# A mixture-of-experts block on one core: attention without loops, expert outputs scattered by token, late routing on VectorE

## The reference, cut to what matters

```
h = x + attention(rmsnorm(x))            # 16 heads of 8 channels, softmax over 1024 keys
out = h + moe(rmsnorm(h))                # 8 experts, top 2 of 8 logits per token, softmax of the two
moe: for each chosen expert e of a token:
       y = (silu(xf @ w1[e].T) * (xf @ w3[e].T)) @ w2[e].T      # 128 -> 256 -> 128
       out += weight * y
```

## Time and profile before

| what | value |
|---|---|
| three runs | 1239.31, 1238.51, 1228.23 us (median 1238.51) |
| the profiled execution | 1228.6 us, of which the span is 1226.8 us |
| PE busy | 1005.9 us, 82% of the span |
| DVE busy | 836.2 us, 68% |
| ACT busy | 666.3 us, 54% |
| POOL busy | 418.3 us, 34% |
| mean granted clock of TensorE | 0.914 |

### The profile page before, as it was taken

One profiled execution on the slowest core, in us unless ns is written; L12 is line 12 of the kernel. 1 busy time (PEld: TensorE's weight loads), 2 busy tenths in 40 slices (PEclk: granted clock), 3 DMA queues, 4 the chain that ended last, 5 costly groups with the idle time before them and its releaser, 6 DMA issues. The chain is left out here.

```text
span 1226.8 us, 21943 instructions
## 1 busy us (share of the span) xinstructions
PE 1005.9 (82%) x5592; PEld 472.9 (39%) x5592; DVE 836.2 (68%) x1286; ACT 666.3 (54%) x1382; POOL 418.3 (34%) x767
## 2 busy tenths in 40 slices
PE   0156666999999999999999999999999968777850
PEld 0034442333333344344344344434443235554530
DVE  5667658789888778888888888888884013232552
ACT  1001111577777677777777777777776534333320
POOL 6103310010110143433433523524522434644576
PEclk9978776899999989999999999999998579988985
DMA  8954566010100110100101101101100012212342
GB/s 269 383 190 137 137 172 172 1 36 10 36 26 10 37 28 10 44 25 20 43 11 33 43 10 35 43 10 35 44 1 2 17 36 64 73 50 70 96 130 71
DMA packets 61944, 81.56 MB, mean 66 GB/s; under 512 B 8512, under 2 KB 39488, under 8 KB 61504
## 3 DMA queue, kind: packets, MB, share of 16 engines
q1 hardware_dynamic: 45808, 51.93, 14.8%
q10 hardware_dynamic: 11984, 20.59, 4.6%
q0 software_dynamic: 4096, 8.40, 2.3%
HBM read 32.12 MB, written 48.23 MB: 65 GB/s over the span
## 5 line engine op out<-in xcount | busy, mean ns | idle before, releaser
L1084 DVE TENSOR_REDUCE smax<-ps 128x2 f32<-128x1024 f32 x512 | 601.7, 1220 | 96.7 <-PE ps L1273 93.5
L853 ACT ACTIVATE prob<-ps 128x512 f32<-128x512 f32 x1024 | 528.8, 603 | 160.2 <-PE ps L1322 157.5
L1322 PE MATMUL ps<-qpack,kpack 34*128 34x512 f32 x1024 | 383.8, 458 | 23.6 <-ACT prob L853 11.7
L1273 PE MATMUL ps<-kpack,qpack 34*128 34x512 f32 x1024 | 314.2, 452 | 10.0 <-DVE smax L1084 9.3
L1322 PEld LDWEIGHTS ps<-qpack,kpack 34*128 34x128 f32 x1024 | 172.9, 189 | 297.2 <-ACT prob L853 250.2
L1332 PE MATMUL ps<-prob,vpad 128*32 128x512 f32 x2048 | 284.7, 629 | 0.0
L1273 PEld LDWEIGHTS ps<-kpack,qpack 34*128 34x128 f32 x1024 | 138.3, 189 | 41.3 <-DVE smax L1084 28.5
L450 POOL MEMSET qpack<- 2x2048 f32 x32 | 57.6, 1799 | 207.9 <-PE ps L1322 205.2
L1190 DVE TENSOR_TENSOR prob<-ps,prob 128x256 f32<-128x256 f32 x80 | 33.9, 424 | 104.9 <-ACT prob L906 104.0
L1498 PE MATMUL ps<-w,ws 128*128 x160 | 89.1, 642 | 15.3 <-ACT ws L899 14.5
L906 ACT ACTIVATE prob<-ps 128x256 f32<-128x256 f32 x80 | 30.8, 385 | 86.3 <-PE ps L1498 86.3
(11 more groups left out here) (211 smaller groups left out, 881.4 us busy)
## 6 DMA issues: line engine op xcount, KB each, us to landing
by_expert_rows<-prob ACTq DMA_DIRECT2D x4, 4864.0 KB, 30.9
q_parts<-qk SPq DMA_DIRECT2D x32, 256.0 KB, 3.8
k_parts<-qk SPq DMA_DIRECT2D x32, 256.0 KB, 4.0
kpack<-k_parts SPq DMA_DIRECT2D x32, 256.0 KB, 3.9
qpack<-q_parts SPq DMA_DIRECT2D x64, 128.0 KB, 3.3
vall<-by_expert_rows SPq DMA_DIRECT2D x80, 64.0 KB, 1.8
by_expert_rows<-vall SPq DMA_DIRECT2D x80, 64.0 KB
w<-w_t SPq DMA_DIRECT2D x3, 1024.0 KB, 10.1
```

Of the source, the lines that this page charges most:

```text
L853: act.activation(prob[:, v % RING, :], bank(col_bank(pos, kind)), ACT.Exp).then_inc(col_free, 1)
L1084: dve.tensor_reduce(smax[:, half, :, pair, qt, kh], ps[:, first:first + 2, :], AX_X, ALU.max).then_inc(row_free, 1)
L1273: ins = pe.matmul(bank(first + par), qpack[r:r + ROWS, slot, half, pair, qt * P:(qt + 1) * P], kpack[r:r + ROWS, slot, pair, kh * HALF:(kh ...
L1322: pe.matmul(bank(col_bank(pos, kind)), kpack[r:r + ROWS, slot, head // 2, kt * P:(kt + 1) * P], qpack[r:r + ROWS, slot, half, head // 2, : ...
```

## The change

Attention: the loops on PE, ACT and DVE become Python loops, so that all 16 quads are straight code. SP and POOL keep theirs. In the fronts of blocks 0 to 5 POOL takes the first guess of the reciprocal root itself with a power operation and does two Newton steps; `seed` on DVE goes.

Rows in DRAM: a scattered row gets four more columns (528 bytes in place of 512). Two of them say in which line of the token order (2 x token) its result belongs, and which slot the token's second row has. The zero fill of `by_expert_rows` grows with it and marks the rows that nothing fills.

Expert stage: for each group DVE works out from these two columns the 512 destination lines (`find_dest`, four small instructions and two waits at j % 4 == 1). POOL scatters each finished tile to `by_token` with one indirect DMA (`scatter_y`), from a `y_nat` of eight groups. SP no longer writes tiles; it waits for `dest_ready` as well before it loads the next group. `save_x` on ACT moves from j % 4 == 3 to j % 4 == 2.

Late fronts (blocks 6 and 7): DVE does the residual add straight from PSUM, the sum of squares, the root, the scaling, and the top two by `max` and `max_index`, in ten steps of each block between the tiles' own work (`FRONT_AT`). POOL keeps the staging, one add, `place_tokens` and the scatter (`place_late`, after `scatter_y` of tiles 21 and 33) and the second table (after that of tile 37).

End: SP loads the two rows of each token of a block with one direct DMA of 512 KB (`load_y`), and DVE combines two tiles of tokens per expert tile from j = 67 on, the last eight after the last expert tile.

```diff
-            with loop(pe, 0, 2) as i:
+            for i in range(2):
                 pe_pair(i, ("plain", "plain"), "even")
-            with loop(pe, 0, EARLY - 1) as t:
+            for t in range(EARLY - 1):
                 pe_pair(t + 2, ("even", "odd"), "even", t)
...
-        LATE = {2: ("turn_a", 6), 5: ("project", 6), 14: ("turn_h", 6), 17: ("logits", 6), 18: ("turn_a", 7),
-                22: ("ranks", 6), 23: ("project", 7), 33: ("turn_h", 7), 36: ("logits", 7), 41: ("ranks", 7)}
+        LATE = {1: ("turn_a", 6), 3: ("project", 6), 5: ("turn_a", 7), 7: ("project", 7), 13: ("turn_h", 6),
+                15: ("logits", 6), 20: ("turn_h", 7), 22: ("ranks", 6), 24: ("logits", 7), 34: ("ranks", 7)}
-        LATE_SEED = {12: 6, 31: 7}
-        COMBINE = 60
+        COMBINE = 67
...
+            def scatter_y(j):
+                group, k = j // 4, j % 4
+                gp.wait_ge(dest_ready, group + 1)
+                gp.wait_ge(y_saved, j + 1)
+                gp.indirect_dma_start(
+                    by_token, bass.IndirectOffsetOnAxis(ap=dest[:, group, k:k + 1], axis=0),
+                    y_nat[:, group % YR, k * H:(k + 1) * H], None).then_inc(y_out[group % YR], 16)
...
+            for j in range(TILES_T):
+                if j == 6:
+                    add_h(EARLY)
+                if j == 12:
+                    add_h(EARLY + 1)
+                if j == 22:
+                    place_late(EARLY, done, h_rows)
+                if j == 34:
+                    place_late(EARLY + 1, done + PLACE_STEPS, h_last)
+                if j == 38:
+                    gp.wait_ge(scattered, 16 * 8 * BLOCKS)
+                    make_table(1, CAP_B, TILES_A, TILES_B, done + 2 * PLACE_STEPS)
+                scatter_y(j)
...
-                if j % 4 == 3 and j + 1 < TILES_T:
+                if j % 4 == 2 and j + 2 < TILES_T:
                     save_x(j // 4 + 1)
...
+            def find_dest(group, before):
+                dve.wait_ge(x_loaded[group % 3], 16 * 4 * (group // 3 + 1))
+                if group == GROUPS_A:
+                    dve.wait_ge(f_tab, 6)
+                first, second, rows = x_nat[:, group % 3, :, H], x_nat[:, group % 3, :, H + 1], row_of[:, 4 * group:4 * group + 4]
+                dve.tensor_tensor(same[:, 0, :], second, rows, ALU.is_equal)
+                dve.scalar_tensor_tensor(same[:, 1, :], first, float(SPARE), rows, ALU.is_ge,
+                                         ALU.mult).then_inc(dve_self, 1)
+                dve.wait_ge(dve_self, before + 1)
+                dve.tensor_tensor(same[:, 0, :], same[:, 0, :], first, ALU.add).then_inc(dve_self, 1)
+                dve.wait_ge(dve_self, before + 2)
+                dve.tensor_tensor(dest[:, group, :], same[:, 0, :], same[:, 1, :], ALU.add).then_inc(dest_ready, 1)
...
+                if j % 4 == 1 and j + 3 < TILES_T:
+                    find_dest(j // 4 + 1, start + count[0])
+                    count[0] += 2
+                for t, places in FRONT_AT.items():
+                    if j in places:
+                        next(fronts[t])
+                if j >= COMBINE:
+                    for _ in range(2):
+                        if combined < 4 * EARLY:
+                            combine(combined, start + count[0])
+                            count[0] += 1
+                            combined += 1
```

More of the change, by code:

```diff
@@ L422, in _ @@
                              xacc[:, t * 4:t * 4 + 4, :]).then_inc(stored, 16)
+            sp.wait_ge(scattered, 16 * 8 * EARLY)
+            sp.wait_ge(f_tab, 3)
+            for group in range(3):
+                load_x(group)
+            for group in range(GROUPS - 3):
+                if group + 3 == GROUPS_A:
+                    sp.wait_ge(scattered, 16 * 8 * BLOCKS)
+                    sp.wait_ge(f_tab, 6)
+                sp.wait_ge(x_turned, group + 1)
+                sp.wait_ge(dest_ready, group + 1)
+                load_x(group + 3)
+            written(GROUPS_A)
+            for t in range(EARLY):
+                load_y(t)
+                if t >= 3:
+                    store(t - 3)
+            for t in range(EARLY - 3, EARLY):
+                store(t)
+            written(GROUPS)
+            for t in range(EARLY, BLOCKS):
+                load_y(t)
+            for t in range(EARLY, BLOCKS):
+                store(t)
             sp.wait_ge(stored, 16 * BLOCKS)
@@ L706, in late, with add_h, place_late @@
                 return LATE_POS[name, t] + 1
-            first, second = done, done + PER_FRONT
+            def add_h(t):
+                gp.wait_ge(late_sum, t - EARLY + 1)
+                gp.tensor_tensor(xacc[:, t * 4:t * 4 + 4, :], xacc[:, t * 4:t * 4 + 4, :], zres[:, t * 4:t * 4 + 4, :],
+                                 ALU.add).then_inc(late_added, 1)
+            def place_late(t, base, rows):
+                gp.wait_ge(f_hot, t + 1)
+                gp.wait_ge(late_norm, t - EARLY + 1)
+                if t > EARLY:
+                    gp.wait_ge(scattered, 16 * 8 * t)
+                place_tokens(t, base, lambda: gp.wait_ge(fr_free, late("ranks", t)), rows)
+                gp.sem_inc(late_placed, 1)
+                scatter(rows)
@@ L712, in _ @@
[L712 to L714 removed]
+            gp.wait_ge(fr_full, late("turn_a", EARLY))
             stage_attention(EARLY + 1)
[L716 to L722 removed]
@@ L723, in _ @@
-            pick_two(EARLY + 1, second)
-            place_tokens(EARLY + 1, second, lambda: gp.wait_ge(fr_free, late("ranks", 7)))
-            scatter(EARLY + 1)
-            done += 2 * PER_FRONT
-            make_table(1, CAP_B, TILES_A, TILES_B, done)
-            def fetch(t):
-                if t >= 4:
-                    gp.wait_ge(added, t - 3)
-                for s in range(2):
-                    gp.indirect_dma_start(
-                        y_two[:, t % 4, s, :], None, by_expert_rows,
-                        bass.IndirectOffsetOnAxis(ap=slot_all[:, s, t:t + 1], axis=0)).then_inc(y_in[t % 4], 16)
@@ L886, in _ @@
                 exp_group(g, 0, 0, "plain")
-            with loop(act, 0, 2) as i:
+            for i in range(2):
                 act_pair(i, ("plain", "plain"), "even")
-            with loop(act, 0, EARLY - 1) as k:
+            for k in range(EARLY - 1):
                 act_pair(k + 2, ("even", "odd"), "even", k)
@@ L1156, in dve_quad @@
                     split_maxima(0, following + (pair_pos(15) + 1), own + 3)
-                    maxima(16, 20, following)
-                    if t is not None:
-                        seed(t, own + 5)
-                    maxima(20, PAIRS - 2, following)
-                    finish_o(quad, 1, following + (O_LATE + 1), row_banks(O_LATE), own + (5 + extra))
+                    maxima(16, PAIRS - 2, following)
+                    finish_o(quad, 1, following + (O_LATE + 1), row_banks(O_LATE), own + 5)
                 else:
@@ L1165, in dve_quad @@
                     finish_o(quad, 1, O_LAST + 2, FINAL_BANK, own + 3)
-            with loop(dve, 0, 2) as i:
+            for i in range(QUADS // 2 - 1):
                 own = i * (2 * PER_QUAD) + start
@@ L1209, in _ @@
+            FRONT_AT = {EARLY: (5, 6, 7, 8, 9, 10, 11, 17, 18, 19), EARLY + 1: (8, 9, 10, 12, 13, 14, 15, 30, 31, 32)}
+            fronts = {t: late_front(t) for t in FRONT_AT}
+            count[0] = 0
+            step = chain(start)
             combined = 0
+            find_dest(0, start)
+            count[0] += 2
             for j in range(TILES_T):
```

266 lines of the change are left out of this document (153 added, 113 removed).

## The result

The changed kernel takes 1158.34 us (median of 1193.93, 1156.49, 1160.14 and 1156.53) beside 1233.37 of the kernel before (four runs, 1227.61 to 1239.31). The ratio is 0.9388, 95% interval 0.9326 to 0.9449: faster. 1188 us had been predicted, with a range of 1174 to 1214, so the sign was right and the size too small.

What follows compares the result with a forecast made beforehand. PE was taken to bound attention, groups of four tiles the experts, POOL's fetches the end. First product at 993.8, table 1105.1, last output 1168.1, span 1186.1, plus 1.8 gave 1187.9, rounded 1188 us; range 1174 to 1214.

Steps and rivals of the forecast that it cites:

- Part 1: Attention: straight code removes only the second loop's stall, -7.0 us, block 5's placing adds 1.0; first expert product at 993.8.
- my own list of what would show it: Signs of right or wrong, among them no attention half quad over 25 us before the last quad, no long ACT issue wait.
- Rival B: Attention: straight code stalls three engines, 18 stalls at 2.4 to 7.0 us; time 1231 to 1314; chance 0.07.
- D: Attention: the loops bring nothing, the wait at 421 us returns elsewhere; time 1195; counted within the forecast's 0.57.
- rival E: Last quad keeps its clock, 33.9 us near 23, time 1177, or the table's wait is short, 1178; chance 0.11.
- Part 2: Expert groups: earlier `save_x` saves 0.9 us, so 6.85 us a group; front steps on DVE add 4 us in all.
- Rival C: Late fronts on DVE cost their full 14 us before tile 53; time 1195; counted within the forecast's 0.57.
- Part 3: Expert stage: POOL becomes late, 61.3 us of work from tile 21; second table at 1105.1, product 55 at 1112.3.
- about 12: Expert stage: the wait for the second table grows from 8.3 us to about 12, holding DVE in `find_dest(14)`.
- rival A: POOL pays 1.6 us per scatter instead of 1.25; time 1205; chance 0.20 together with other dearer pieces.
- Part 4: Last 25 tiles: tile 67 at 1134.8, then two combines make 2.5 us a tile; last output saved at 1168.1.
- Part 5: End: last scatter to 1170.7, loads 6.0 us, combines 6.2, last store 3.2; span 1186.1.

Runs made afterwards that it cites:

- scatter_late: Changed kernel with POOL starting the row scatters of blocks 0 to 4 only after the pair's second refill of the values; 1157.19 us, 0.9398 of the kernel before.
- before_again: The kernel before, unedited, run again for a trace from the same chip; 1243.54 us.
- again_b: The changed kernel, unedited, as yardstick on a chip that pauses; 1268.68 us, 0.9472 of the kernel before.
- savex_back: Changed kernel with ACT's `save_x` put back to j % 4 == 3; 1274.39 us, 0.9461 of the kernel before, on a chip that pauses.
- table_early70_c: Changed kernel with POOL's placing of blocks 6 and 7 and second table earlier, combines from tile 70; 1269.29 us, 0.9477 of the kernel before.
- again: The changed kernel, unedited, run once more; 1158.52 us, 0.9404 of the kernel before.

## Why the prediction was wrong

**Part 1 failed**, at its ground: "a steady loop costs nothing and straight code gains nothing by itself". The 24.5 us that this was read from the earlier trace rows belong to the half quad in which the straight code begins; the fair comparison was the next one, 21.8 against 22.4 and 22.5. PE's timeline of the kernel before has this line in the half quad of 24.5:

```profile
890.54 0.49 PE L1322 MATMUL ps<-qpack,kpack 34*128 34x512 f32 x1 [0.76 <-ACT prob L853]
```

ACT is in straight code there already, and its groups of four exponentials stand as far apart as in the same half quad of `scatter_late`, but for one that takes 3.42 us in place of 2.61. This single delay of 0.8 us, just behind the end of the loop, made the row as long as that of a looped half quad and hid the gain. Ahead of the first product the change brought 29.7 us, not 6.0:

| term | predicted | measured |
|---|---|---|
| 7 plain half quads, 22.4 to 21.8 | 0 | 4.2 |
| half quad at the second loop, 31.4 to 23.6 | 7.0 | 7.8 |
| the next 20 half quads, 469.2 to 455.6 | 0 | 13.6 |
| last quad, 55.8 to 54.2 | 0 | 1.6 |
| start, and last reciprocal to first product | -1.0 | 2.5 |

So the error is a missing term, 27 half quads at 0.66 us, and not the stall that I had costed. In the steady half quads the loss is a register step of 0.08 us that is paid once in each of the 8 groups of four exponentials.

The Trainium skill, in Runtime: NRT & Kernel Launch (Instruction fetch mechanics), has a taken branch stall when its target isn't at hand, and gives this as one reason why kernels prefer full unrolling. The loops' back edges show no such cost here: at each of the five (319.3, 509.9, 603.7, 697.4 and 791.3 us) ACT's next exponential follows without idle time, and DVE idles 0.3 us at most. The stall of 2.58 us comes 10 us behind the branch that leaves the first loop (408.95), in the first pass through the second loop's body. In the DMA records of the trace an 8 KB packet of instructions arrives inside it, at 420.1 us, and so it is in `before_again` (418.2, stall from 417.1 to 419.8). But straight code brings more such packets on the two queues that the page shows (86 in `scatter_late`, 56 before) and has no stall, so the stall's cause is not shown.

By my own list of what would show it: no "issue" of over 2 us stands on ACT in attention up to the last quad of `scatter_late`, and none of its half quads of attention before the last quad is over 25 us. Rival B (unrolled code stalls) did not come at all, and D (the stall comes again elsewhere) neither. The first half of the last quad kept more of its clock (30.2 us at 0.71 for 33.9 at 0.60), a third of what rival E put on it, and the second half lost 2.1 us of this again.

**Part 2 held.** A group takes 6.70 us, predicted 6.85. The first four groups take 8.5, 10.0, 8.2 and 9.3 us, with late items on PE and front steps on DVE. Product 21 comes 44.7 us after the first; 45.3 had been worked out. The 20.2 us window of before has no successor. Rival C (the front steps cost in full) is out.

**Part 3 held, with its sign.** POOL's timeline of `scatter_late` around the second table, and DVE's:

```profile
1072.09 0.96 POOL L788 DMA_INDIRECT by_token<-wk,vall  x1 [0.31 <-issue]
1073.07 0.22 POOL L701 TENSOR_TENSOR counts<-run,ebase 128x8 f32<-128x8 f32 x1
...
1082.22 0.20 POOL L721 CAST qk<-qk 128x24 int32<-128x24 f32 x1
```

```profile
970.05 0.42 DVE L1229 TENSOR_TENSOR prob<-ps,prob 128x256 f32<-128x256 f32 x1 [3.96 <-ACT prob L968]
...
1086.52 0.20 DVE L1245 TENSOR_TENSOR vall<-vall,qk 128x4 f32<-128x4 f32 x1 [15.47 <-DMA vall<-by_expert_rows]
...
1089.81 0.42 DVE L1229 TENSOR_TENSOR prob<-ps,prob 128x256 f32<-128x256 f32 x1 [1.93 <-ACT prob L968]
```

The table is complete at 1082.42, which is 112.4 us after the first product (111.3 predicted), and product 55 follows 7.4 us later (7.2). DVE stands 15.47 us in `find_dest` of group 14, named ahead; "about 12" was too short, because tile 53 came 100.2 us after the first product and not 102.9, and the table 1.1 us later than predicted. Behind the table the scatters stand 1.26 us apart whatever DVE does, so rival A's 1.6 us did not come, and of its two grounds neither the second wait nor DVE's instructions with two inputs from SBUF showed a cost.

**Part 4 was right up to tile 67** (141.4 us after the first product, 141.0 predicted) and mis-sized behind it. A tile with two combines takes 1.96 us, and 2.5 to 2.7 only behind tiles 69 and 73, where DVE has a `find_dest` as well: 12 tiles took 24.9, not 30.0. The term "0.42 + 0.42 + 4 x 0.354 + 0.2" added durations; instructions in a row on DVE start 0.27 to 0.39 us apart while each lasts 0.35.

**Part 5 was mis-sized by the load.** The end of `scatter_late`, on ACT, POOL, SP's queue and DVE:

```profile
1139.43 0.28 ACT L976 ACTIVATE wk<-ps 128x128 f32<-128x128 f32 x1 [1.25 <-PE ps L1636]
...
1140.47 0.96 POOL L788 DMA_INDIRECT by_token<-wk,vall  x1 [0.57 <-issue]
...
1142.88 0.92 SPq L432 DMA_DIRECT2D kpack<-by_token  x2
...
1146.71 0.35 DVE L1258 SCALAR_TENSOR_TENSOR xacc<-kpack,share,xacc 128x128 f32<-128x128 f32 x1 [8.16 <-DMA kpack<-by_token]
...
1151.65 0.35 DVE L1261 SCALAR_TENSOR_TENSOR xacc<-kpack,share,xacc 128x128 f32<-128x128 f32 x1
```

From product 79 (1136.3) to the end it is 18.4 us, 21.3 predicted. The first combine starts 3.8 us after the loads' first issue (6.0 taken, from rows of four loads at once), the sixteen instructions take 5.3 (6.2), and the store 2.7 (3.2). From product 79 to the loads' first issue it is 6.6 us (5.9).

The cases of the forecast were laid out around Part 1's sum, so the range inherited its error: nothing in it reached more than 14 us below, while the one row that I had read as "straight code gains nothing" carried 18. Two sums of the rivals are off too, without bearing on this. From the table to the last output Part 4 has 63 us (1105.1 to 1168.1) and not 56, so rival A comes to about 1203. And loops over two and five pairs use their code again for five pairs, not six, so rival B has 15 stalls and not 18.

## What to carry to other kernels

When two stretches of "the same work" are to be compared, take all steps of the row, by the instruction counts in the window, and leave out those in which a loop or a stretch of straight code begins. A serial engine's chain, worked out from rows (here POOL's 61.3 us from the scatter of tile 21 to the table, measured 61.6), is a better ground for a forecast than a comparison of two averages.

## What the runs showed that was not expected

**Chips that pause.** On two of the chips, 4 and (in two rounds) 11, both kernels ran 9 to 12% longer (kernel before 1346 to 1371 us, changed kernel 1269); on chips 8 and 2 they did not. There PE, ACT and DVE stand still together, for 3 to 5 us at the first pause in the traces of `again_b` and `savex_back`. The timeline of `savex_back`, POOL's first and sixth indirect DMA of a row scatter, and then the three engines:

```profile
480.91 1.23 POOL L689 DMA_INDIRECT by_expert_rows<-qk,slots  x1 [1.01 <-issue]
...
487.50 0.96 POOL L689 DMA_INDIRECT by_expert_rows<-qk,slots  x1 [0.30 <-issue]
...
492.07 2.08 ACT L913 ACTIVATE prob<-ps 128x512 f32<-128x512 f32 x4 [4.55 <-remote]
492.11 2.36 DVE L1141 TENSOR_REDUCE smax<-ps 128x2 f32<-128x1024 f32 x2 [4.06 <-remote]
...
492.72 0.79 PE L1435 MATMUL ps<-qpack,kpack 34*128 34x512 f32 x1 [4.01 <-issue]
```

In `again_b` the row scatters start at 480.3, 580.2, 689.2, 798.4 and 907.5 us and the pauses at 488.1, 588.6, 697.7, 806.8 and 916.0, each 7.8 to 8.5 us later, while the scatters are still going on. The first holds PE for 3.1 us, the other four for about 1 us each. Each is followed by 17 to 41 us at 1.2 GHz, so a half quad of 21.8 or 23.6 takes up to 31.8. The expert stage has them too, during long runs of scatters (DVE 8.28 us in `table_early70_c`). They come with loops and without, before the change and after. Their cause is open: that they follow the scatters is a coincidence in time that no run here took apart.

**The clock can fall without a gap.** The windows of `again` before and after such a fall:

```profile
530.00:553.00 23.00, 22.73 (x145) 9.95 (x145) 19.58 (x22) 17.69 (x37) 5.43 (x8) 1.00 0.13 36
553.00:573.50 20.50, 20.50 (x86) 9.23 (x79) 11.09 (x11) 10.20 (x23) 9.35 (x33) 0.50 0.04 14
```

PE is busy 22.73 of 23.00 us and then runs 20.5 us at 1.2 GHz. The same place, about 3 us after the eight short matmuls of a `logits` item (8 columns each, 0.96 us in all, at 550.1), shows it in the profiled execution of the changed kernel; `scatter_late` has the same item and no fall. The kernel before shows such a fall too: in `before_again` the clock drops at 476.9 us, with no gap on PE of over 0.12 us in the half quad, which takes 31.6 us at a clock of 0.69. What decides is open.
